# Two-stage layer kernel: HHT gets 36 slots, and the next tile's first four m6 chunks are issued ahead of the quantisation

## The reference

```python
def act_quant(x):
    scale = 127.0 / jnp.clip(jnp.max(jnp.abs(x), axis=-1, keepdims=True), 1e-05)
    q = jnp.clip(jnp.round(x * scale), -128.0, 127.0) / scale
    ...
def bitlinear(x, w, b):
    xq = act_quant(rmsnorm(x))
    wq = weight_quant(w)                 # -1, 0, 1 times a scale
    return jnp.einsum('bsd,fd->bsf', xq, wq) + b
h = bitlinear(x, w1, b1)                 # 1024 -> 4096
h = jax.nn.gelu(h, approximate=False)
return bitlinear(h, w2, b2)              # 4096 -> 1024

x = x + _L0_attn_ref(_layernorm(x, axis=-1), ...)
x = x + _L0_ffn_ref(_layernorm(x, axis=-1), ...)
```

## Time and profile before

| | us |
|---|---|
| Time of the kernel, median of 3 runs | 7444.55 (7443.64 to 7451.11) |
| Profiled execution | 7485.33 |
| Its span on the slowest core (core 2) | 7483.6 |
| Spans of the 8 cores | 7412.6 to 7483.6 |
| VectorE busy | 4166.7 (56%) |
| TensorE matmuls busy | 3219.0 (43%) |
| ScalarE busy | 927.2 (12%) |
| DMA, share of 16 engines, all queues | 8.5% |

### The profile page before, as it was taken

One profiled execution on the slowest core, in us unless ns is written; L12 is line 12 of the kernel. 1 busy time (PEld: TensorE's weight loads), 2 busy tenths in 40 slices (PEclk: granted clock), 3 DMA queues, 4 the chain that ended last, 5 costly groups with the idle time before them and its releaser, 6 DMA issues.

```text
span 7483.6 us, 67091 instructions; the slowest of 8 cores (7412.6 to 7483.6 us)
## 1 busy us (share of the span) xinstructions
PE 3219.0 (43%) x19024; PEld 2087.1 (28%) x19024; DVE 4166.7 (56%) x9489; ACT 927.2 (12%) x1723; POOL 5.2 (0%) x8
## 2 busy tenths in 40 slices
PE   3654556655556621144344344344334434434432
PEld 2433334433334410022122122122212212212222
DVE  2555655655666555645555655655555555565556
ACT  1111111111111100021111111111111111111110
POOL 0000000000000000000000000000000000000000
PEclk8666666766667755555555565555555655556556
DMA  6000000000000034300000000000000000000000
GB/s 111 15 15 20 15 15 16 16 21 20 15 15 16 16 108 160 112 6 1 14 15 15 0 15 15 0 14 14 0 14 15 11 4 15 14 0 14 14 0 12
DMA packets 120956, 173.98 MB, mean 23 GB/s; under 512 B 5748, under 2 KB 105236, under 8 KB 118548
## 3 DMA queue, kind: packets, MB, share of 16 engines
q1 hardware_dynamic: 115412, 152.20, 6.7%
q0 software_dynamic: 5184, 17.50, 1.5%
HBM read 145.22 MB, written 41.96 MB: 25 GB/s over the span
## 4 chain that ended last, share of the span: by engine, by line
DVE 42%; PE 29%; issue 11%; ACT 8%; DMA 7%; DVEq 2%; SPq 0%; ACTq 0%
DVE DH L850 9%; PE psH L731 7%; PE psO L863 6%; ACT HHT L741 4%; DVE MH L846 4%; DMA WQ<-f2T 3%; DVE PR L738 3%; PE psRow L260 2%; DVEq L935 2%; PE PaA L395 2%; PE PaB L401 2%; DMA X<-xT 2%; ACT HS L747 2%; DVE DHP L553 2%; PE PaC L395 1%
## 5 line engine op out<-in xcount | busy, mean ns | idle before, releaser
L750 PE MATMUL psRowH<-HS,ONEB 128*1 128x256 bf16 x512 | 190.4, 372 | 2293.3 <-ACT HS L747 2293.3
L731 PE MATMUL psH<-XQ,f1q 128*128 128x256 bf16 x4096 | 966.4, 418 | 10.0 <-ACT IABC L155 10.0
L850 DVE SCALAR_TENSOR_TENSOR DH<-MH,DH 128x512 f16<-128x512 f16 x1024 | 708.8, 692 | 106.9 <-DVE MH L846 0.7
L750 PEld LDWEIGHTS psRowH<-HS,ONEB 128*1 128x1 bf16 x512 | 40.5, 79 | 2524.1 <-issue 2524.1
L741 ACT ACTIVATE HHT<-PR,B1S,THR 128x256 f16<-128x256 f32 x512 | 307.0, 600 | 2732.1 <-DVE PR L738 2731.9
L731 PEld LDWEIGHTS psH<-XQ,f1q 128*128 128x128 bf16 x4096 | 530.6, 141 | 343.7 <-issue 152.0
L738 DVE TENSOR_TENSOR PR<-psH,IABC 128x256 f32<-128x256 f32 x512 | 215.7, 421 | 652.4 <-PE psH L731 652.4
L863 PE MATMUL psO<-HQT,f2q 128*128 128x256 bf16 x4096 | 519.1, 291 | 134.4 <-DVE HQT L854 127.1
L863 PEld LDWEIGHTS psO<-HQT,f2q 128*128 128x128 bf16 x4096 | 420.8, 104 | 229.0 <-issue 157.1
L761 DVE TENSOR_TENSOR MX<-MX,HHT 128x256 f16<-128x256 f16 x496 | 144.9, 292 | 417.3 <-ACT HHT L741 417.3
L417 PE MATMUL psF<-GV,w2sb 128*128 128x256 bf16 (+1 forms) x2816 | 360.8, 284 | 20.4 <-DVE GV L409 10.9
(11 more groups left out here) (162 smaller groups left out, 4479.4 us busy)
## 6 DMA issues: line engine op xcount, KB each, us to landing
WQ<-f1T SPq DMA_DIRECT2D x16, 2048.0 KB, 8.6
WQ<-f2T SPq DMA_DIRECT2D x64, 512.0 KB, 3.6
X<-xT SPq DMA_DIRECT2D x16, 1024.0 KB, 6.6
xoh<-XOUT SPq DMA_DIRECT2D x16, 1024.0 KB, 4.4
XO<-xoh SPq DMA_DIRECT2D x16, 1024.0 KB, 6.7
outT<-XO SPq DMA_DIRECT2D x16, 1024.0 KB, 5.3
xqh<-XQS SPq DMA_DIRECT2D x128, 64.0 KB, 1.6
XQ<-xqh SPq DMA_DIRECT2D x16, 512.0 KB, 6.6
```

What stands on the lines that cost most here:

```text
L731: mm = e.matmul(pH[:], f1q[:, c, fc * 128:(fc + 1) * 128], XQ[:, c, :], start=(c == 0), stop=(c == NCHUNK - 1))
L850: f=lambda e, s=s: e.scalar_tensor_tensor(out=DH[:], in0=MH[:], scalar=-s, in1=DH[:], op0=ALU.mult, op1=ALU.add))
```

## The change

HHT is enlarged from 32 to 36 slots and used as a ring: chunk fc of tile `it` goes to slot (32 it + fc) mod 36. The first four chunks of tile `it + 1` are issued after its loads and ahead of pair 0 of tile `it`. Pair g is then followed by chunks 2g + 4 and 2g + 5, and pairs 14 and 15 by none. HQT keeps its 32 places. The operations, their shapes and their number are the same.

```diff
-    HHT = sbA(s2, "HHT", [128, F2CHUNK, TT], FP16)
+    HHT = sbA(s2, "HHT", [128, 36, TT], FP16)
+    hslot = lambda it, fc: (F2CHUNK * it + fc) % 36
...
@@ p2_m6_chunk
-        kHc = "HHT:%d" % fc
+        hs_ = hslot(it, fc)
+        kHc = "HHT:%d" % hs_
...
         ctx.op("act", r=[kPR, "THR", "B1S"], w=[kHc],
-               f=lambda e, fc=fc, PR=PR: e.activation(
-                   out=HHT[:, fc, :], in_=PR[:], func=AF.Gelu,
+               f=lambda e, fc=fc, PR=PR, hs_=hs_: e.activation(
+                   out=HHT[:, hs_, :], in_=PR[:], func=AF.Gelu,
                    bias=B1S[:, fc:fc + 1], scale=THR[:, 4:5]))
...
@@ p2_quant_pair
-        sl = slice(2 * g, 2 * g + 2)
-        kH0, kH1 = "HHT:%d" % (2 * g), "HHT:%d" % (2 * g + 1)
+        s0 = hslot(it, 2 * g)
+        sl = slice(s0, s0 + 2)
+        slq = slice(2 * g, 2 * g + 2)
+        kH0, kH1 = "HHT:%d" % s0, "HHT:%d" % (s0 + 1)
...
-               f=lambda e, sl=sl: e.tensor_tensor(out=HQT[:, sl, :], in0=Y1H[:],
-                                                  in1=DH[:], op=ALU.subtract))
+               f=lambda e, slq=slq: e.tensor_tensor(out=HQT[:, slq, :], in0=Y1H[:],
+                                                    in1=DH[:], op=ALU.subtract))
...
@@ the loop over the tiles
         if it + 1 < NT:
             p2_loads(it + 1)
+            for fc in range(4):
+                p2_m6_chunk(it + 1, fc)
         for g in range(F2CHUNK // 2):
             p2_quant_pair(it, g)
             if g == 4:
                 p2_invh_bcast(it)
                 if it + 1 < NT:
                     p2_load_xo(it + 1)
-            if it + 1 < NT:
-                p2_m6_chunk(it + 1, 2 * g)
-                p2_m6_chunk(it + 1, 2 * g + 1)
+            if it + 1 < NT and 2 * g + 5 < F2CHUNK:
+                p2_m6_chunk(it + 1, 2 * g + 4)
+                p2_m6_chunk(it + 1, 2 * g + 5)
```

More of the change, by code:

```diff
@@ L746, in p2_m6_chunk @@
         ctx.op("act", r=[kHc], w=[khs],
-               f=lambda e, fc=fc, hsq=hsq: e.activation(out=hsq[:], in_=HHT[:, fc, :],
-                                                        func=AF.Square))
+               f=lambda e, hs_=hs_, hsq=hsq: e.activation(out=hsq[:], in_=HHT[:, hs_, :],
+                                                          func=AF.Square))
         ctx.op("pe", r=[khs, "onesbf"], w=["ph:row"],
@@ L753, in p2_m6_chunk @@
             ctx.op("dve", r=[kHc], w=["MX2"],
-                   f=lambda e: e.tensor_copy(out=MX2[:], in_=HHT[:, 0, :]))
+                   f=lambda e, hs_=hs_: e.tensor_copy(out=MX2[:], in_=HHT[:, hs_, :]))
             ctx.op("dve", r=[kHc, "MX2"], w=["MX2"],
-                   f=lambda e: e.scalar_tensor_tensor(out=MX2[:], in0=HHT[:, 0, :],
-                                                      scalar=-1.0, in1=MX2[:],
-                                                      op0=ALU.mult, op1=ALU.max))
+                   f=lambda e, hs_=hs_: e.scalar_tensor_tensor(out=MX2[:], in0=HHT[:, hs_, :],
+                                                               scalar=-1.0, in1=MX2[:],
+                                                               op0=ALU.mult, op1=ALU.max))
         else:
             ctx.op("dve", r=[kHc, "MX2"], w=["MX2"],
-                   f=lambda e, fc=fc: e.tensor_tensor(out=MX2[:], in0=MX2[:],
-                                                      in1=HHT[:, fc, :], op=ALU.max))
+                   f=lambda e, hs_=hs_: e.tensor_tensor(out=MX2[:], in0=MX2[:],
+                                                        in1=HHT[:, hs_, :], op=ALU.max))
             ctx.op("dve", r=[kHc, "MX2"], w=["MX2"],
-                   f=lambda e, fc=fc: e.scalar_tensor_tensor(out=MX2[:], in0=HHT[:, fc, :],
-                                                             scalar=-1.0, in1=MX2[:],
-                                                             op0=ALU.mult, op1=ALU.max))
+                   f=lambda e, hs_=hs_: e.scalar_tensor_tensor(out=MX2[:], in0=HHT[:, hs_, :],
+                                                               scalar=-1.0, in1=MX2[:],
+                                                               op0=ALU.mult, op1=ALU.max))
     def p2_stats(it, pend=None):
```

## The result

The changed kernel takes 7607.82 us, the median of ten runs (7593.19 to 7678.97), against 7458.56 us for the kernel before, the median of ten runs too. The ratio is 1.0199, with a 95% interval of 1.0168 to 1.0230. That is +148 us (+125 to +172) on 7458.56, where the forecast's sum was +149.3. The absolute forecast of 7594 us is 14 us low, and the kernel before has its median 14 us higher over ten runs than over the first three.

The account below looks back on a forecast made before the run. Waits bound the kernel, from TensorE's queue order (L750 ahead of the next chunk's matmuls). Per turn 8.50 + 15.70 - 14.07 = +10.13 us; total +149.3 on the median 7444.55 gives 7593.9 us, 8 in 10 within 7565 to 7627.

Parts of the forecast that it names:

- Slots cost nothing: HHT buffer: four extra slots add no instruction and change no shape, so cost nothing.
- The rounds stay: Rounds 0 to 13 of a tile: order kept, so priced at the old 14.07 us each.
- PR(0) does not move: Turn of a tile: the first chunk's PR keeps its time, since the iah load chain sets it.
- The lead: Chunks 0 to 3 ahead of Q0: chunks 2 and 3 run with no Q to hide behind, +8.50 us a turn.
- The tail: Tile's end: Q14 and Q15 run bare, +15.70 us, against one round fewer, -14.07 us.
- The sum: Whole kernel: +10.13 us a turn over 15 turns, first turn -2.66 us, total +149.3 us.
- The two halves of the mechanism: Each turn: Q0 loses its shadow (7.8 us) and one more group of m6 matmuls is exposed (2.3 us).
- The psO start at no cost: First psO matmuls after 15.7 us of idle TensorE: priced at nothing; +25 us if the old start were warm.
- B: TensorE's clock rises to 2.4 GHz through the rounds: 7330 us, chance 0.02; lead only warm: 7535 us, 0.04.
- C: VectorE takes a ready instruction past a waiting one, so Q0 fills the lead's wait: 7444 us, chance 0.02.
- D: Lead works as distance, odd PRs in the rounds never wait: 462 us less, 7132 us, chance 0.02.
- E: Costlier than forecast: cold psO start (+25) or dear lead chunks (+33), up to 7652 us; beyond the range 0.04.

Follow-up runs that it names:

- Experiment 6: Kernel before with each chunk's one-row sum-of-squares matmul issued behind the next chunk's eight matmuls; ratio 0.9181 to the kernel before.
- experiment 1: Changed kernel without the lead: 36 slots alone, old order of the queues; ratio 1.0008 to the kernel before.
- Experiment 4: Changed kernel with the next tile's loads, their broadcast and the copy to IABC issued ahead of the statistics; ratio 0.9976 to the kernel before.
- experiment 3: Changed kernel with a lead of two chunks instead of four; ratio 1.0163 to the kernel before.
- experiments 2: Changed kernel with Q0 issued ahead of the four-chunk lead; ratio 1.0042 to the kernel before.
- experiments 7 and 10: 7: changed kernel with late one-row matmul, 0.9316; 10: changed kernel with early loads, late one-row matmul and late maximum, 0.8568; both against the kernel before.
- the early loads: Next tile's loads, broadcast and copy to IABC issued ahead of the statistics; alone in the kernel before, ratio 0.9947.
- Experiment 8: Kernel before with early loads, late one-row matmul, and each chunk's maximum behind the PR two chunks on; 6329.45 us against 7454.91, ratio 0.8489.

## Why the prediction was right

*What bounds the kernel: shown.* Waits inside the round, made by the order of TensorE's queue. Experiment 6 moves one instruction and takes 2.2 us from each round (534.4 us of distance over 15 tiles of 16 rounds), with the buffers and the clock of the rounds as they were.

*Slots cost nothing: shown* by experiment 1.

*The rounds stay: confirmed.* 13.96 us as the mean of rounds 0 to 13 in 14 tiles, against 14.00 for rounds 1 to 14 in the kernel before; I had used 14.07, one tile's mean with the longer last round in it. (A Q has fourteen VectorE instructions, not the thirteen of my count; no time rests on it.)

*PR(0) does not move: confirmed.* It comes 11.89 us after the start of the last evacuation, as a mean over 14 turns, and 11.93 before. Experiment 4 shows why.

*The lead: +8.50 forecast.* From PR(0) to the first Q behind it are 15.80 us after (mean of 14) against 7.37: +8.43.

*The tail: +15.70 - 14.07 = +1.63 forecast.* From that Q to the next statistics step are 210.97 us after and 210.38 before, +0.59; and the statistics step now starts 0.2 us ahead of psO instead of 0.25 behind it, so that from it to the next PR(0) are 0.39 us more. So +0.98, and 0.65 less than forecast. The last round of a tile before was not 14.07 but 14.43 us, with the wait for L750 in it, and this wait fell away.

*The sum: 10.13 a turn forecast,* 8.43 + 0.98 = 9.4 measured; the first turn 7.47 forecast, 7.78 measured (244.79 against 237.01 us between the two statistics steps). 14 x 9.4 + 7.78 = 139.4. That is what the order explains, 10 us less than the sum of 149.3, and most of it is the tail. That the ratio's +148 and the +149.5 of the eight cores' means nevertheless agree with the sum to 1.5 us is luck: by the means, the stretch from the first psO matmul to the last evacuation takes 39.8 us against 39.1, 0.7 a turn, for which the forecast had nothing. In this stretch the cores of one execution differ too: in the kernel before, 14 times the way from the statistics step to PR(0) are 696 to 725 us by core, and 14 times the rest of the turn 3048 to 3051. Why is open. It is not the idle time of TensorE ahead of psO, since experiment 4 has that too and takes 39.2.

*The two halves of the mechanism,* "Q0 loses its shadow (7.8) and one more group is exposed (2.3)", are shown apart: 7.4 to 7.5 by experiment 3, and 1.8 to 2.6 by experiments 2 and 3.

*The psO start at no cost: confirmed in the profile.* The first 32 weight loads take 5.13 us there, and 5.07 in the last tile of the kernel before after 127 us of idle time. Over all 15 turns of the eight cores, the 33rd psO matmul starts 5.80 us after the first, and 5.81 before, where TensorE comes to them from the rounds. The rule of the Trainium skill on gaps between bursts (TensorE: Matmul & The Clock Gate, "HAM oscillation") had nothing to take here.

*Rivals.* B (clock): 0.50 in the rounds and 1.87 to 1.89 us for a group; one group of the 18, in experiment 4, does run at the high level, but VectorE is not free for it sooner. C: Q0, ready, stands behind a PR that waits for 11.24 us. D: not in the changed kernel, and by experiments 7 and 10 not where TensorE may run ahead either. E: the psO start was not dearer, and the lead's chunks came 4.21 and 4.23 us apart.

## What to carry to other kernels

Where engines take their work in a written order, as here, a larger distance between producer and consumer may bring nothing unless the instruction that really blocks the queue is moved; look for the small dependent one (here a one-row matmul) that stands ahead of large independent ones. Before moving work ahead of other work, ask what that other work was covering: Q0 filled a load chain, and its place had no other filler. When the cover must go, take away first what it covered, as the early loads do. And before a difference of a few us a turn is read from one core, look at the other seven.

## What the runs showed of the hardware

The distance between two VectorE instructions depends on whether the second needs the first's result. In experiment 8 an instruction of 0.42 us is followed 0.34 us after its start by one that does not need its result (4199.10 to 4199.44, 4199.82 to 4200.16). Inside Q, where each step reads the last one's result, such an instruction and the next stand 0.52 to 0.53 us apart; in the kernel before:

```profile
4651.40 0.42 DVE L831 TENSOR_TENSOR Y1H<-HHT,G2BH 128x512 f16<-128x512 f16 x1
...
4651.92 0.43 DVE L835 CAST HI<-Y1H 128x512 int32<-128x512 f16 x1
```

Interleaving the chunks therefore saved a little beyond the waits. In experiment 6 the two chunks of a round take 4203.74 - 4199.75 = 3.99 us; without the waits for the gelu, 0.80 and 0.87, that is 2.32 us, and experiment 8 takes 2.13. The difference is 0.2 us a round, in which each PR is followed by the maximum of an earlier chunk 0.34 us after its start, 0.08 ahead of its end. That this makes the 0.2 us is argued from these rows; no experiment tests it alone.
